# A rewritten graph-attention stage: POOL only scatters, deviation on ACT, mask and scores summed in PSUM

## What is computed

```python
x = x + gat(layernorm(x), adj)
#   h = n @ W;  e = leaky_relu(s1[:, None] + s2[None, :], 0.2)   s1 = h @ a1, s2 = h @ a2
#   e = where(adj > 0, e, -9e15);  elu(softmax(e) @ h)
x = x + experts(layernorm(x))
#   scores = n @ Wg.T + bg;  top two of 8, softmax of the two as weights
```

## Time and profile before

| | us |
|---|---|
| runs | 1358.58, 1364.79, 1369.54 |
| median | 1364.79 |
| profiled execution, time | 1351.87 |
| its span | 1350.0 |

### The profile page before, as it was taken

One profiled execution on the slowest core, in us unless ns is written; L12 is line 12 of the kernel. 1 busy time (PEld: TensorE's weight loads), 2 busy tenths in 40 slices (PEclk: granted clock), 3 DMA queues, 4 the chain that ended last, 5 costly groups with the idle time before them and its releaser, 6 DMA issues. The chain is left out here.

```text
span 1350.0 us, 27968 instructions
## 1 busy us (share of the span) xinstructions
PE 1025.9 (76%) x6752; PEld 825.6 (61%) x6753; DVE 797.4 (59%) x3187; ACT 563.3 (42%) x1364; POOL 623.2 (46%) x686
## 2 busy tenths in 40 slices
PE   3666656379999999289988977979851989989930
PEld 3555445279999999245545544645430989988930
DVE  4776777445555555347767957768552444434418
ACT  3555555233333333146545644545430333333315
POOL 3577677724444554301335244253354355555540
PEclk8666666589999999789989989989965999999975
DMA  4223231222222221222203112040004322222229
GB/s 119 63 80 88 74 97 38 69 66 70 66 67 64 68 66 53 59 63 63 72 23 91 41 57 86 8 132 12 20 32 90 77 73 81 73 76 76 65 82 322
DMA packets 126205, 98.73 MB, mean 73 GB/s; under 512 B 33864, under 2 KB 115400, under 8 KB 126152
## 3 DMA queue, kind: packets, MB, share of 16 engines
q1 hardware_dynamic: 105536, 61.24, 16.7%
q0 software_dynamic: 17152, 35.29, 7.9%
q10 hardware_dynamic: 3464, 1.59, 0.6%
HBM read 55.44 MB, written 42.62 MB: 73 GB/s over the span
## 5 line engine op out<-in xcount | busy, mean ns | idle before, releaser
L1433 POOL DMA_INDIRECT result<-e_y,e_ids x280 | 274.6, 981 | 278.8 <-DVE e_y L1547 115.0
L1462 PE MATMUL e_ps_h<-e_xT,e_up_of 128*128 128x128 f32 x2240 | 290.1, 280 | 24.7 <-issue 21.8
L1462 PEld LDWEIGHTS e_ps_h<-e_xT,e_up_of 128*128 128x128 f32 x2240 | 271.4, 195 | 32.6 <-issue 29.6
L1477 PE MATMUL e_ps_y<-w_sb,e_hT 128*128 x1664 | 214.1, 278 | 5.5 <-issue 3.3
L1477 PEld LDWEIGHTS e_ps_y<-w_sb,e_hT 128*128 128x128 f32 x1664 | 200.7, 194 | 6.6 <-issue 6.2
L375 POOL DMA_INDIRECT queue<-g_q_rows,g_q_slots x128 | 129.8, 1014 | 77.9 <-DVE g_q_gap L320 38.4
L375 POOL DMA_INDIRECT queue<-a_r_rows,a_r_slots x128 | 129.0, 1008 | 63.9 <-issue 44.2
L1501 ACT ACTIVATE e_hT<-e_ps_h,b_sb 128x128 f32<-128x128 f32 x272 | 78.3, 377 | 139.6 <-remote 93.5
L1540 DVE TENSOR_SCALAR e_hT<-e_ps_h,b_sb 128x128 f32<-128x128 f32 x272 | 76.5, 343 | 84.6 <-remote 78.2
L1529 DVE COPY e_up_of<-w_sb 128x512 f32 x280 | 109.1, 430 | 5.5 <-issue 3.2
L1556 DVE TENSOR_TENSOR e_hT<-e_ps_h,e_gate 128x512 f32<-128x512 f32 x72 | 49.6, 689 | 101.7 <-ACT e_gate L1510 66.9
(11 more groups left out here) (218 smaller groups left out, 1892.4 us busy)
## 6 DMA issues: line engine op xcount, KB each, us to landing
e_xq<-queue SPq DMA_DIRECT2D x280, 64.5 KB
g_y<-result SPq DMA_DIRECT2D x16, 512.0 KB
o_y<-result SPq DMA_DIRECT2D x16, 512.0 KB, 5.3
w_sb<-w SPq DMA_DIRECT2D x48, 128.0 KB
result<-e_y,e_ids POOLq DMA_INDIRECT x280
x_res<-x SPq DMA_DIRECT2D x16, 256.0 KB
w_sb<-w SPq DMA_DIRECT2D x16, 256.0 KB
out<-x_res SPq DMA_DIRECT2D x16, 256.0 KB, 4.6
```

Of the source, the lines that this page charges most:

```text
L1433: pool.indirect_dma_start(out=result, out_offset=bass.IndirectOffsetOnAxis(ap=ids[at_down.k][:, t, :].bitcast(U32), axis=0), in_=y[at_down ...
L1462: last = pe.matmul(ps_h[b][:, t, q * P:(q + 1) * P], up_of[at_up.k % 4][:, t, q * P:(q + 1) * P], xT[at_up.k % 4][:, t, :], start=True, st ...
L1477: last = pe.matmul(ps_y[b][:, t * D:(t + 1) * D], hT[at_down.k % 4][:, t, q * P:(q + 1) * P], down[:, bass.ds(e * (chunks * P) + q * P, P) ...
```

## The change

The attention stage is written anew; the other stages stay as they are.
- POOL has nothing in its body but the eight scatters of g4.
- The inverse deviation is made on ACT as exp(-0.5 ln(v + eps)), two 128x4 activations for each of the two normalisations, both from one preloaded function set. DVE makes the shift from it in one operation.
- Both terms of the attention scores and the mask are summed in PSUM: two fp32 products with 256 columns, eight with 64 columns of weights and 64 moving columns, and an identity matmul in bf16 that adds a mask of -2^55. ACT copies the sum to `e`; DVE's addition of s1 and of the mask go.
- h gets a column of ones, so that the product with h yields the row sum of `pbd`; DVE's sum goes and the reciprocal reads PSUM. ACT's copy of h subtracts 1 and the exponential adds 1 in its exponent's argument, so the elu needs one operation less on DVE.
- Routing on DVE: both marks, both picks and both slots in one operation each, no casts; the ranks take 5 matmuls instead of 14 and stand behind the projection; the weights of the two experts are made once after the loop, from the gaps of all groups.
- The second normalisation goes straight into the row buffer, of which one copy is made instead of two. Input, row and slot buffers are four deep, and the loop body has four steps (`staged`, `TURN` 4). SP loads four groups ahead, and padding waits for a semaphore of POOL's first fills.

The lines removed are the bodies printed above; the added ones that matter:

```diff
+def staged(eng, body):
+    def step(i, j):
+        groups = [Group(i, j - lag) for lag in range(5)]
+        if type(i) is int:
+            groups = [g if 0 <= g.s < NG else None for g in groups]
+        body(*groups)
+    for j in range(TURN):
+        step(0, j)
+    with eng.Fori(1, NG // TURN) as i:
+        for j in range(TURN):
+            step(i, j)
+    for j in range(4):
+        step(NG // TURN, j)
...
+                    wait(pool, VK, "slots", g4.s)
+                    wait(pool, AC, "rows", g4.s)
+                    alone(pool, c)
+                    for k in range(TOPK):
+                        for t in range(G):
+                            pool.indirect_dma_start(
+                                out=c.queue0,
+                                out_offset=bass.IndirectOffsetOnAxis(ap=slots[g4.b][:, k, t:t + 1], axis=0),
+                                in_=rows[g4.b][:, k, t, :], in_offset=None).then_inc(queued[g4.b], 16)
...
+                    v.reciprocal(halves(rinv[:].unsqueeze(2)), half_o[:, :, :, D:D + 1]).then_inc(VU.sem, 1)
+                if g0:
+                    v.wait_ge(arrived[g0.b], 32 * g0.turn + 32)
+                    alone(v, c)
+                    stats(norm1, VN1, g0.s)
+                if g2:
+                    wait(v, VU, "rinv", g2.s)
+                    wait(v, AZ, "elu", g2.back(1))
+                    v.tensor_tensor(halves(z[:]), half_o[:, :, :, 0:D], halves(bc(rinv[:], D)),
                                     ALU.mult).then_inc(VU.sem, 1)
...
                 if g1:
...
+                    wait(v, AE, "e", g1.s)
                     v.scalar_tensor_tensor(out=e[:], in0=e[:], scalar=0.2, in1=e[:], op0=ALU.mult,
                                            op1=ALU.max).then_inc(VA.sem, 1)
...
+                if g0:
+                    aggregate(norm1, VN1, g0.s)
                 if g1:
                     wait(v, VA, "lrelu", g1.s)
...
                     v.tensor_reduce(rowmax[:], e[:], AX.X, ALU.max).then_inc(VA.sem, 1)
                 if g0:
...
+                    if type(g0.s) is int and g0.s == 0:
+                        copy_products()
+                    if type(g0.s) is not int or g0.s >= 2:
+                        wait(v, QX, "s", g0.back(2))
+                    v.tensor_scalar(neg[g0.b % 2][:], adj_sb[g0.b][:], 0.0, NEG, ALU.is_le, ALU.mult).then_inc(VM.sem, 1)
                 if g1:
                     wait(v, VA, "max", g1.s)
                     v.tensor_tensor(e[:], e[:], bc(rowmax[:], N), ALU.subtract).then_inc(VA.sem, 1)
+                if g0:
+                    shift(norm1, VN1, AN1, g0.s)
                 if g3:
...
+                    wait(v, QR, "scored", g3.s)
+                    v.tensor_tensor(score[:], scores_ps.rearrange("p (t e) -> p t e", t=G),
+                                    gb_sb[:, None, :].to_broadcast([P, G, E0]), ALU.add).then_inc(VS.sem, 1)
+                    v.tensor_copy(rows[g3.b][:, :, :, D:ROW].bitcast(I32),
+                                  c.ids[:, :, bass.ds(g3.s * G, G)].unsqueeze(3)).then_inc(VS.sem, 1)
+                if g2:
+                    wait(v, VU, "z", g2.s)
+                    xs = c.x[:, bass.ds(g2.s * G, G), :]
+                    v.scalar_tensor_tensor(out=xz[:], in0=z[:], scalar=-1.0, in1=xs,
+                                           op0=ALU.max, op1=ALU.add).then_inc(VU.sem, 1)
+                if g3:
+                    wait(v, VS, "scores", g3.s)
+                    alone(v, c)
+                    for t in range(G):
+                        last = v.max(top[:, t, :], score[:, t, :])
                     last.then_inc(VS.sem, 1)
...
+                if g2:
+                    wait(v, VU, "xz", g2.s)
+                    wait(v, AZ, "elu", g2.s)
+                    v.scalar_tensor_tensor(out=xs, in0=elu[:], scalar=1.0, in1=xz[:],
+                                           op0=ALU.min, op1=ALU.add).then_inc(VU.sem, 1)
                 if g3:
...
+                    wait(v, VS, "top", g3.s)
+                    alone(v, c)
+                    for t in range(G):
+                        last = v.max_index(where[:, t, :], top[:, t, :], score[:, t, :])
+                    last.then_inc(VS.sem, 1)
+                if g2:
+                    wait(v, VU, "x1", g2.s)
+                    alone(v, c)
+                    stats(norm2, VN2, g2.s)
+                if g3:
+                    wait(v, VS, "where", g3.s)
+                    v.tensor_tensor(hot[:], c.iota_e[:, None, None, 0:E0].to_broadcast([P, TOPK, G, E0]),
+                                    bc(where[:, :, 0:TOPK].rearrange("p t k -> p k t"), E0),
+                                    ALU.is_equal).then_inc(VS.sem, 1)
+                if g2:
+                    aggregate(norm2, VN2, g2.s)
+                if g3:
+                    v.tensor_tensor(gap[:, bass.ds(g3.s * G, G)], top[:, :, 1], top[:, :, 0], ALU.subtract)
+                    wait(v, VS, "hot", g3.s)
+                    v.tensor_tensor(both[:, 0:G, :], hot[:, 0, :, :], hot[:, 1, :, :], ALU.add).then_inc(VS.sem, 1)
+                if g2:
+                    shift(norm2, VN2, AN2, g2.s)
+                if g3:
+                    carry = c.carry[:, 0:E0]
+                    wait(v, QK, "ranked", g3.s)
+                    wait(v, VK, "carried", g3.back(1))
+                    v.tensor_tensor(rank[:], ranks_ps[:, 0:G * E0].rearrange("p (t e) -> p t e", t=G),
+                                    carry[:, None, :].to_broadcast([P, G, E0]), ALU.add).then_inc(VK.sem, 1)
+                    wait(v, VK, "ranked", g3.s)
+                    v.tensor_tensor(carry, ranks_ps[:, G * E0:(G + 1) * E0], carry, ALU.add).then_inc(VK.sem, 1)
+                    v.tensor_tensor(pick[:], hot[:], rank[:, None, :, :].to_broadcast([P, TOPK, G, E0]),
+                                    ALU.mult).then_inc(VK.sem, 1)
+                    wait(v, VK, "pick", g3.s)
+                    with nc.allow_low_precision(reason="one term of each sum is not zero, a whole number"):
+                        v.tensor_reduce(slots[g3.b][:], pick[:], AX.X, ALU.add).then_inc(VK.sem, 1)
...
+            act.preload_act_table_set("natural_log_exp_and_others")
...
+            def inverse_std(m, V, A, s):
+                wait(act, V, "agg", s)
+                act.activation(m.log[:], m.mv[:, :, 1], ACT.Ln, bias=eps[:]).then_inc(A.sem, 1)
+                wait(act, A, "log", s)
+                act.activation(m.rstd[:], m.log[:], ACT.Exp, scale=-0.5).then_inc(A.sem, 1)
+            def normalise_to(dst, m, s):
+                for t in range(G):
+                    last = act.activation(dst[:, t, 0:D], c.x[:, s * G + t, :], ACT.Identity,
+                                          bias=m.shift[:, t:t + 1], scale=m.rstd[:, t:t + 1])
+                return last
 
             def body(g0, g1, g2, g3, g4):
                 if g2:
...
+                    wait(act, VU, "z", g2.s)
+                    wait(act, VU, "x1", g2.back(1))
+                    act.activation(elu[:], z[:], ACT.Exp, bias=1.0).then_inc(AZ.sem, 1)
+                if g0:
+                    inverse_std(norm1, VN1, AN1, g0.s)
                 if g3:
...
+                    wait(act, QR, "turned", g3.s)
+                    act.activation(rT[:], ps_r[:], ACT.Copy).then_inc(AR.sem, 1)
                 if g1:
                     wait(act, VA, "centred", g1.s)
+                    wait(act, QA, "turned", g1.back(1))
+                    alone(act, c)
                     for q in range(2):
...
+                        cells = slice(q * N, (q + 1) * N)
+                        last = act.activation(pbd[cells, :, q * N:(q + 1) * N], e[cells, :, :], ACT.Exp)
                     last.then_inc(AA.sem, 1)
                 if g0:
+                    wait(act, VN1, "shift", g0.s)
                     wait(act, QX, "turned", g0.back(1))
...
+                    alone(act, c)
+                    normalise_to(xn, norm1, g0.s).then_inc(AN1.sem, 1)
                 if g1:
...
+                    wait(act, QA, "turned", g1.s)
                     act.activation(pT[:], ps_p[:], ACT.Copy).then_inc(AA.sem, 1)
                 if g0:
                     wait(act, QX, "turned", g0.s)
...
+                    act.activation(xnT[:], ps_t[:], ACT.Copy).then_inc(AT.sem, 1)
+                if g3:
+                    wait(act, AN2, "normed", g3.s)
+                    act.activation(rows[g3.b][:, 1, :, 0:D], rows[g3.b][:, 0, :, 0:D], ACT.Copy).then_inc(AC.sem, 1)
                 if g2:
...
+                    inverse_std(norm2, VN2, AN2, g2.s)
+                    wait(act, VN2, "shift", g2.s)
+                    if type(g2.s) is not int or g2.s >= TURN:
+                        act.wait_ge(queued[g2.b], 16 * TOPK * G * g2.turn)
+                    alone(act, c)
+                    normalise_to(rows[g2.b][:, 0, :, :], norm2, g2.s).then_inc(AN2.sem, 1)
                 if g0:
                     wait(act, QX, "h", g0.s)
...
```

(41 more changed lines are left out.)

324 lines of the change are left out of this document (127 added, 197 removed).

## The result

| | before | after |
|---|---|---|
| median, us | 1361.7 (1357.3 to 1369.5, 4 runs) | 1391.7 (1386.9 to 1394.1, 4 runs) |
| ratio after / before | | 1.020 (1.014 to 1.026) |
| profiled execution: time, span, us | 1351.9, 1350.0 | 1386.9, 1385.1 |

The account below looks back on a forecast made before the run. No engine full; POOL's list (about 14.0 us) and the DVE-ACT-PE ring bound the 14.8 us step within a microsecond. Stage 51.9 + 146.4 + 43.8 = 242.1 against 271.6; 1364.8 - 29.5 = 1335.3 us, range 1310 to 1358.

Parts of the forecast that it names:

- twelve steps: Attention stage between first scatters of group 0 and group 12: 12.2 us each, 146.4 us, instead of 14.8 each.
- semaphores of PE: Attention step: 0.5 us added to 11.7 for PE's late semaphores, seen in front of L303 and L740.
- fill: Attention stage up to its first scatter: 51.9 us, 3.9 later than before.
- tail: Attention stage from group 12's first scatter to SP's last padding store: 43.8 us instead of 45.7.
- Rival 2: Late PE semaphores and four-step loop boundaries eat the gain: step 13.9 us, 1358 us, no measurable change; chance 0.16.
- A term at nothing that wasn't: ACT's logarithm and exponential hide behind DVE's maximum and subtraction, costing nothing; without that cover 0.5 us a step.
- The prediction's warning: Forecast wrong above all if something counted as hidden sets the step: ACT's copy of h, or DVE reaching z late.
- POOL's part: POOL loses both inverse deviations, 3.6 us a step, leaving a floor of 10.4 us and a slot wait of about 1.8.
- The ring, edit by edit: DVE-ACT-PE chain between successive row-maximum subtractions: 12.9 us at half clock, 10.45 at full, 11.7 with half the steps at each.
- rival 3: PE becomes the bound: 64x64 score passes cost like 128-wide ones, 1.85 us more per step, 1381 us; chance 0.05.
- Rivals 3 and 4: The fourth: ln and exp need different function sets on ACT, reloading tables each step, 14.8 us a step, 1373 us; chance 0.04.
- The clock: PE's granted clock over the attention stage's steady part: from 0.63 to about 0.75, half of the steps at each level.

Follow-up runs that it names:

- e14: After unchanged, run again in surroundings where before takes about 1260 us: 1224.6 us, 0.972 times before.
- e2: After with each step's eight scatters replaced by POOL copies into a large buffer, all 128 scatters issued behind the ring: 1483.0 us, 10.97 us a step.
- e5: Before with each step's eight scatters replaced by POOL copies, all 128 issued behind the ring, POOL keeping its powers and products: 12.70 us a step.
- e10: After with POOL waiting for the newest group's normalised x between its fourth and fifth scatter, about 1360 us surroundings: 1343.9 us, 0.991 times before.
- e7: Before with only the inverse deviation moved to ACT and the shift to DVE, eight scatters in one run, about 1260 us surroundings: 1263.7 us, 1.002 times before.
- e15: After with eight plain transfers a step on POOL's queue in place of the scatters, which all come behind the ring: 1466.8 us.
- e1: Before unchanged, measured once more for a second profile: 1377.3 us.

## Why the prediction was wrong

| step of the first stage, us | forecast | after, loud | after, quiet (e14) |
|---|---|---|---|
| first scatter | 51.9 | 47.5 | 47.9 |
| twelve steps (one) | 146.4 (12.2) | 191.3 (15.94) | 131.2 (10.93) |
| ring without scatters | 11.7 | 10.97 (e2) | |

- **The step that failed** is the sentence "To that I add 0.5 for semaphores of PE that arrived up to 2.7 us after its records end", "for which I find no cause". That term is 5.0 us a step in the loud surroundings in which the kernel was measured (15.94 against 10.97 in e2), ten times as much, and nothing in quiet ones (10.93 in e14). I carried over a wait of before as a constant, though its cause sat in what the change rearranges. The miss in the twelve steps, 12 x 3.74 = 45 us, is all of the stage's miss: SP's last padding store ends at 286.6 instead of 242.1, +44.5, with the fill 4.4 us better and the tail 4.1 worse.
- **What the trace of before would have shown.** I read two rows of its "remote" waits. Two more stood in the same view, from 48 us on:

```profile
ACT a_h L768 <- remote: 8.4, 2, 4.5
DVE a_e L676 <- remote: 5.7, 5, 1.6
```

  Together the four are 38.6 us, up to 4.5 us each; the 0.5 us a step that I added is 6 us over twelve steps. Their size, and that they stood on both DVE and ACT, asked for a cause; of the 28 late updates of PE that this trace records from 50 to 215 us, 25 belong to instructions that end while POOL issues scatters. Rival 2 had the right mechanism ("nothing in the trace explains those waits"), but added 1.0 us a step, though its own sentence has 1.5, and called no change; 1.5 would have made it 14.4 us a step, still less than the measured 15.94.
- **Why before suffers less.** Its step of 14.8 is 2.1 us above its ring without scatters (12.70, e5) and 0.8 above POOL's own list of 14.0; after is 5.0 above its ring. Two differences stand in the traces: before scatters in runs of three, two and three, after in one run of eight; and in before only PE's updates are late, in after DVE's too. Cutting the run in two (e10) brings the 5.0 down to 2.6 (13.59). How much of before's lateness was hidden behind POOL's own work, which I removed, the runs don't tell.
- **A term at nothing that wasn't.** The logarithm and exponential on ACT "cost nothing as long as DVE needs its 1.2 us there". In the old ring, this part of the change alone costs 1.1 us a step (13.80 in e7 against 12.70 in e5). In the new ring their cost isn't measured by itself; the ring as a whole came out below the forecast all the same.
- **The prediction's warning** ("if the step is set by something I count as hidden") was right in form, but named the wrong things: in the 178 us of after ACT's copy of h waited 0.6 us for PE, and ACT 1.4 us for DVE's z.
- **POOL's part: right.** No power in the stage, scatters 1.3 apart; its floor of 10.4 us is close to the quiet step of 10.9. The wait for slots was to be 1.8 us and was 5.8 on the mean (63.3 us in 11 places).
- **The ring, edit by edit: right within 0.8 us.** 11.7 us forecast without the late semaphores, 10.97 measured in e2. DVE: 7.7 us a step forecast; e14 has 85.18 us in the 120 us above, 7.8 a step. The scores block, which rival 3 made decisive, in after at 0.61 of the clock (90 to 180 us, by shape; busy, mean ns):

```profile
L939 PE MATMUL a_ps_s<-a_wa_wide,a_xnT 128*64 128x64 f32 x96 | 7.9, 285 | 0.0
L934 PE MATMUL a_ps_s<-a_xnT,a_wa_wide 128*64 128x256 f32 x24 | 6.7, 662 | 0.0
...
L942 PE MATMUL a_ps_s<-a_neg,a_ident_b 128*128 128x256 bf16 x6 | 1.9, 320 | 0.0
```

  Sixteen passes in 7.9/6 = 1.32 us, 0.08 each: below my 0.115. With the wide products (1.12) and the mask (0.32) it is 2.8 us, between the forecast's 3.2 at the lower level and 1.6 at the full one. Rivals 3 and 4 are out (there is one table load in the stage).
- **The clock: wrong in loud surroundings, nearly right in quiet ones.** Forecast 0.75 of full over the steady part; it was 0.62, with PE busy 63% of the time, and 0.80 in e14 over 60 to 180 us, with PE busy 74%.
- **Tail.** I held SP's register loads in front of its four padding stores at their 13.49 us; after has them at 12.00. In e14 the same four take 4.04. But they took 3.69 us in e2 and 4.26 in e15 as well, both loud and with the late scatters starting beside them; so what makes them slow isn't shown.
- **The sum.** Where nothing comes late, the change brings 1259.5 - 1224.6 = 34.9 us; the forecast was 29.5. Where updates come late, the two sets that hold both kernels say +30.0 and +11.3 us. The first stage's profiles differ by 10 to 16 us there, about 1%, and that is what the stage explains; the rest of the +30 lies in stages that have no edit, and e1 shows such a shift without any edit. That the quiet gain comes so near the forecast is in part luck: the forecast started from the loud 271.6 us, while the quiet stage of before is about 256 to 264 us by an estimate (its span of 1257.6 less the 994 to 1002 that the later stages take in quiet profiles), and after's is 222.6 where 242.1 was forecast.

## What to carry to other kernels

A wait whose releaser the profile can't name is a cost with a cause; before it goes into a sum as a constant, look what else runs at each of its places, and ask whether the change moves that. Moving work to another engine to relieve one that "bounds" can lengthen the ring that the new engine is part of, as the deviation did here (12.70 to 13.80 us). If GpSimd issues indirect transfers beside a chain of short dependent steps, try to cut its run with a wait on a milestone of that chain: one wait was worth 1.8% here (1343.9 against 1368.2 us), and cost nothing where it wasn't needed.
